# First attention: two groups of heads projected and split, block 1 normalized, before the first scores; the first stack read in halves

## What is computed

```python
def _L0_attn_ref(in_features, Wq, Wk, Wv, Wo):      # 16 heads of 16
    q = split_heads(in_features @ Wq.T)
    k = split_heads(in_features @ Wk.T)
    v = split_heads(in_features @ Wv.T)
    scores = jnp.einsum('bhsd,bhtd->bhst', q, k) * scale
    scores = jnp.where(causal[None, None], scores, -jnp.inf)
    attn = jax.nn.softmax(scores, axis=-1)
    out = jnp.einsum('bhst,bhtd->bhsd', attn, v)
    return out.transpose(0, 2, 1, 3).reshape(B, S, D) @ Wo.T
...
xn = _layernorm(x, axis=-1)
x = x + _L0_attn_ref(xn, ...) + _L0_ffn_ref(xn, ...)     # 8 experts, 2 per token, and a shared one
xn = _layernorm(x, axis=-1)
x = x + _L1_attn_ref(xn, ...) + _L1_ffn_ref(xn, ...)     # a gated linear attention; 8 experts, 2 per token
```

## Time and profile before

| | |
|---|---|
| median of three runs | 1816.02 us (1812.69 to 1818.68) |
| the profiled execution | 1823.78 us, span of its instructions 1821.9 us, mean granted clock 0.942 |
| PE (TensorE, matmuls) busy | 1638.2 us, 90% of the span |
| DVE (VectorE) busy | 869.7 us, 48% |
| ACT (ScalarE) busy | 667.7 us, 37% |
| POOL (GpSimd) busy | 738.1 us, 41% |
| the chain that ended last, by engine | PE 78%, DVE 12%, issue 4% |

### The profile page before, as it was taken

One profiled execution on the slowest core, in us unless ns is written; L12 is line 12 of the kernel. 1 busy time (PEld: TensorE's weight loads), 2 busy tenths in 40 slices (PEclk: granted clock), 3 DMA queues, 4 the chain that ended last, 5 costly groups with the idle time before them and its releaser, 6 DMA issues.

```text
span 1821.9 us, 32039 instructions
## 1 busy us (share of the span) xinstructions
PE 1638.2 (90%) x10912; PEld 1214.3 (67%) x10912; DVE 869.7 (48%) x2492; ACT 667.7 (37%) x1617; POOL 738.1 (41%) x845
## 2 busy tenths in 40 slices
PE   3798988988887999999988578999899999999997
PEld 2344534444443799999755345656899999999997
DVE  3866787667650232322165797988322112222221
ACT  1344444445452122222353334432433333333332
POOL 3122223455551055555542237885233333333332
PEclk8789988989897999999999789999999999999999
DMA  7533433252404122222351255435622222222221
GB/s 203 117 90 95 97 84 76 54 106 64 95 5 163 66 72 72 71 73 70 117 162 58 73 174 117 97 70 123 240 36 36 38 36 39 36 36 35 37 40 22
DMA packets 79739, 149.98 MB, mean 82 GB/s; under 512 B 13125, under 2 KB 61377, under 8 KB 73441
## 3 DMA queue, kind: packets, MB, share of 16 engines
q1 hardware_dynamic: 55040, 110.56, 23.2%
q0 software_dynamic: 24544, 37.38, 9.5%
HBM read 103.05 MB, written 44.45 MB: 81 GB/s over the span
## 4 chain that ended last, share of the span: by engine, by line
PE 78%; DVE 12%; issue 4%; ACT 2%; DMA 2%; POOL 1%; SPq 0%; DVEq 0%; ACTq 0%; POOLq 0%
PE PS L1413 21%; PE PS L1431 20%; PE PS L1299 5%; DVE PS L1717 5%; PE PS L1237 3%; PE PS L1526 3%; PE PS L1378 3%; PE PS L1387 2%; PE PS L1263 2%; PE PS L1617 2%; PE PS L1398 2%; PE PS L1284 2%; PE PS L1325 2%; PE PS L1536 1%; PE PS L1606 1%
## 5 line engine op out<-in xcount | busy, mean ns | idle before, releaser
L1413 PEld LDWEIGHTS PS<-arena 128*128 128x128 f32 x3408 | 400.7, 193 | 15.8 <-DVE arena L1940 4.5
L1413 PE MATMUL PS<-arena 128*128 128x128 f32 x3408 | 407.5, 277 | 3.1 <-DVE arena L1940 3.1
L1431 PE MATMUL PS<-arena 128*128 x1704 | 392.4, 379 | 0.0
L1431 PEld LDWEIGHTS PS<-arena 128*128 128x128 f32 x1704 | 311.6, 190 | 40.2 <-issue 0.2
L1940 DVE COPY arena<-PS 128x256 f32<-128x256 f32 x142 | 60.3, 425 | 413.2 <-PE PS L1398 402.9
L1717 DVE CUSTOM_DVE_ANT_0 PS<-PS,arena 128x512 f32<-128x512 f32 (+3 forms) x512 | 234.2, 524 | 36.2 <-PE PS L1263 36.0
L866 POOL DMA_INDIRECT out<-arena x71 | 111.6, 1572 | 313.6 <-ACT arena L1087 292.5
L1077 ACT ACTIVATE arena<-PS,arena 128x128 f32<-128x128 f32 x568 | 162.4, 368 | 138.2 <-PE PS L1413 138.2
L1016 ACT ACTIVATE arena<-PS 128x512 f32<-128x512 f32 (+1 forms) x256 | 166.9, 704 | 89.0 <-PE PS L1284 87.8
L806 POOL TENSOR_SCALAR_AFFINE_SELECT arena<-arena 128x256 f32<-128x256 f32 x256 | 99.0, 411 | 230.8 <-ACT arena L1016 229.4
L852 POOL DMA_INDIRECT arena<-XN,arena x142 | 142.0, 1000 | 122.8 <-PE PS L1398 81.6
(11 more groups left out here) (237 smaller groups left out, 2058.5 us busy)
## 6 DMA issues: line engine op xcount, KB each, us to landing
arena<-FD SPq DMA_DIRECT2D x32, 512.0 KB
arena<-in_w SPq DMA_DIRECT2D x16, 1024.0 KB
SPL<-arena SPq DMA_DIRECT2D x32, 384.0 KB, 2.6
arena<-SPL SPq DMA_DIRECT2D x32, 384.0 KB, 5.3
XN<-arena SPq DMA_DIRECT2D x16, 512.0 KB, 2.9
arena<-SPL SPq DMA_DIRECT2D x32, 256.0 KB, 6.2
arena<-SUM SPq DMA_DIRECT2D x16, 512.0 KB, 5.1
arena<-in_x SPq DMA_DIRECT2D x8, 512.0 KB, 10.1
```

Of the source, the lines that this page charges most:

```text
L1413: ins = pe.matmul(o, m.now[i % 2][:, c * F + 128 * f:c * F + 128 * f + 128], m.xt[i % 2][:, 128 * c:128 * c + 128], start=(c == 0), stop=( ...
L1431: ins = pe.matmul(to, m.hT[i % len(m.hT)][:, 128 * c:128 * c + 128], m.WD[:, bass.ds(e * (nf * 256) + c * 256, 256)], start=(c == 0), stop ...
```

## The change

Six things change.

1. Before the first `scores` the plan now has the projections and cuts of groups 0 and 1, `stack` 0 and 1, both halves of V of block 0, the logits of block 0, and all layer-norm steps of block 1 up to `logitsT`. Group 2's projections enter the waiting list at once, at idx = -10.
2. What ACT, DVE, POOL and SP do behind a projection (bf16 copy, subtraction and cast, low part, write) is a step of its own, `cut` (n, m). For groups 0 and 1 it stands behind both projections. From group 2 on `with_cuts` places it: behind the next `scores`, or, if earlier, ahead of a second small step after the projection or of a `stack`.
3. All four banks are used by turns until idx = 0 (`two_banks`); from there on 7 and 6. The count that `scoresT` of head 0 waits for follows from it (`exp_first`).
4. `stack` 0 is read in two halves, for heads 0 to 3 and 4 to 7 (twelve DMAs). PE waits for the second half at head 4 (`stk_late`). In every group all six reads now wait for both writes.
5. SP issues the loads of x for blocks 2 to 7 before those of Wo, at the start.
6. Since the layer norm is seven steps ahead, `route` and `scatter` begin seven values of idx earlier.

```diff
--- before.py
+++ after.py
@@ -70,7 +70,6 @@
     ln = ln0_steps()
     for _ in range(2):
         out += next(ln)
-    out.append(("first_banks",))
     waiting = []
 
     def later(rank, parts):
@@ -87,20 +86,26 @@
                     continue
             return
 
-    out.extend([("project", 0, 0), ("project", 0, 1), ("stack", 0), ("clear_meta",)])
-    later(0, [("project", 1, 0), ("project", 1, 1), ("stack", 1)])
-    later(3, [("project_v", 0, 0), ("project_v", 0, 1), ("done",)])
+    for n in range(2):
+        out.extend([("project", n, 0), ("project", n, 1), ("cut", n, 0), ("cut", n, 1), ("stack", n)])
+        out.extend([("project_v", 0, 0), ("project_v", 0, 1)] if n else [("clear_meta",)])
+    while out[-1] != ("logitsT", 1):
+        out += next(ln)
     route = iter([("route", p) for p in range(20)] + [("scatter", i, (k,)) for i in range(NT) for k in range(2)])
     clears = iter([("clear", p) for p in range(4)])
     lnleft = True
     for idx in range(-LEAD, NH + 1):
-        if idx % 8 == 5 and 2 <= (idx + 3) // 8 + 2 < NHB:
+        if idx == 1 - LEAD:
+            later(0, [("project", 2, 0), ("project", 2, 1), ("stack", 2)])
+        if idx % 8 == 5 and 3 <= (idx + 3) // 8 + 2 < NHB:
             later(0, [("project", (idx + 3) // 8 + 2, 0), ("project", (idx + 3) // 8 + 2, 1), ("pause",)])
-        if idx % 8 == 0 and 2 <= idx // 8 + 2 < NHB:
+        if idx % 8 == 0 and 3 <= idx // 8 + 2 < NHB:
             out.append(("stack", idx // 8 + 2))
         if idx == NH - 6:
             out.append(("bias_rows",))
         lead = idx + LEAD
+        if idx == 0:
+            out.append(("two_banks",))
         if 0 <= idx < NH:
             out.append(("scoresT", idx // 8, idx % 8))
             step()
@@ -129,9 +134,34 @@
         step()
     out += list(route)
     out.append(("slots",))
+    return with_cuts(out)
+
+
+def with_cuts(steps):
+
+
+    out, left = [], []
+
+    def flush():
+        out.extend(("cut",) + c for c, _ in left)
+        left.clear()
+
+    for step in steps:
+        small = step[0] in SMALL or step[0] == "values" or step == ("route", 15)
+        if left and (step[0] == "stack" or (small and left[0][1])):
+            flush()
+        out.append(step)
+        if small:
+            left[:] = [(c, True) for c, _ in left]
+        if step[0] == "project" and step[1] >= 2:
+            left.append((step[1:], False))
+        if step[0] == "scores":
+            flush()
+    assert not left
     return out
 
 
+SMALL = ("xt0", "xt1", "logits", "logitsT", "project", "project_v", "maxrow", "scale", "unscaleT", "output")
 CLOSE = ("stack", "maxrow", "unscaleT", "pause", "done")
 
 
@@ -247,11 +277,12 @@
 def attention_banks(order):
 
 
-    uses, ring, first = Uses(), [4, 5, 6, 7], True
+    uses, ring = Uses(), [4, 5, 6, 7]
     for step in order:
-        if step[0] == "first_banks":
-            ring, first = [7, 6], False
-        elif step[0] in ("xt0", "xt1", "logits", "logitsT", "project", "project_v", "maxrow", "scale", "unscaleT", "output"):
+        if step[0] == "two_banks":
+            ring = [7, 6]
+            uses.at[step] = tuple(uses.count[b] for b in (4, 5))
+        elif step[0] in SMALL:
             ring.append(ring.pop(0))
             uses.take(step, ring[-1])
         elif step[0] == "values":
@@ -487,6 +518,7 @@
 
         plan0 = attention_order()
         banks0 = attention_banks(plan0)
+        exp_first = banks0.pop(("two_banks",))
         plan1 = shared_order()
         plan2 = second_order()
         scat_all = 32 * (NT // 4)
@@ -509,6 +541,7 @@
         spl_out = [[sem(f"spl_out{n}{m}") for m in range(2)] for n in range(3)]
         stk_in = [[sem(f"stk_in{n}{m}") for m in range(2)] for n in range(3)]
         max_in = [sem(f"max_in{n}") for n in range(3)]
+        stk_late = [sem(f"stk_late{m}") for m in range(2)]
         v_made, s_made, s_max = sem("v_made"), sem("s_made"), sem("s_max")
         max_cut, max_turned = sem("max_cut"), sem("max_turned")
         const0_set, p_cut = sem("const0_set"), sem("p_cut")
@@ -583,6 +616,8 @@
             x_load(1)
             sp.dma_start(WRV[:, :, :], t["Wg"]).then_inc(wr_in, 16)
             sp.dma_start(WV[:, :, :], t["Wv"]).then_inc(wvo_in, 16)
+            for b in range(2, NB):
+                x_load(b)
             heads = t["Wo"].rearrange("(j r) g n -> j r g n", r=32)
             for g in range(4):
                 lo = 64 * (g % 2)
@@ -596,18 +631,22 @@
                 sp.wait_ge(lo_cut, 2 * n + m + 1)
                 if n >= 3:
                     sp.wait_ge(stk_in[n % 3][m], 48 * (n // 3))
+                if n == 3:
+                    sp.wait_ge(stk_late[m], 48)
                 sp.dma_start(SPL[n % 3, m].rearrange("k p s -> p k s"), PT[m]).then_inc(spl_out[n % 3][m], 16)
 
             def stack(n):
                 for m in range(2):
                     sp.wait_ge(spl_out[n % 3][m], 16 * (n // 3 + 1))
-                    if n >= 3:
-                        sp.wait_ge(st_made, 16 * (n - 2))
-                        sp.wait_ge(s_made, 24 * (n - 2))
-                    parts = SPL[n % 3, m].rearrange("k (d j) s -> k d (j s)", j=8)
-                    for sl, part, many in SLOTS[m]:
-                        dst = STK[n % 3][m][16 * sl:16 * (sl + many), :, :].rearrange("p j s -> p (j s)")
-                        sp.dma_start(dst, parts[part:part + many]).then_inc(stk_in[n % 3][m], 16)
+                if n >= 3:
+                    sp.wait_ge(st_made, 16 * (n - 2))
+                    sp.wait_ge(s_made, 24 * (n - 2))
+                for lo, hi in ((0, 4), (4, 8)) if n == 0 else ((0, 8),):
+                    for m in range(2):
+                        parts = SPL[n % 3, m].rearrange("k (d j) s -> k d (j s)", j=8)
+                        for sl, part, many in SLOTS[m]:
+                            dst = STK[n % 3][m][16 * sl:16 * (sl + many), lo:hi, :].rearrange("p j s -> p (j s)")
+                            sp.dma_start(dst, parts[part:part + many, :, S * lo:S * hi]).then_inc(stk_late[m] if lo else stk_in[n % 3][m], 16)
 
             def maxrow(n):
                 bk, use = banks0["maxrow", n]
@@ -643,13 +682,10 @@
             for kind, *a in plan0:
                 if kind == "norm":
                     norm0(*a)
-                elif kind == "project":
+                elif kind == "cut":
                     split_out(*a)
                 elif kind == "stack":
                     stack(*a)
-                    if a[0] == 0:
-                        for b in range(2, NB):
-                            x_load(b)
                 elif kind == "maxrow":
                     maxrow(*a)
                 elif kind == "bias_rows":
@@ -1256,6 +1292,9 @@
                 h = 8 * n + j
                 pe.wait_ge(stk_in[n % 3][0], 48 * (n // 3 + 1))
                 pe.wait_ge(stk_in[n % 3][1], 48 * (n // 3 + 1))
+                if h == 4:
+                    pe.wait_ge(stk_late[0], 48)
+                    pe.wait_ge(stk_late[1], 48)
                 for i in (3, 2, 0, 1):
                     w, o = 128 * (i + 1), OFF[i]
                     if h and i != 0:
@@ -1280,7 +1319,7 @@
                     if h:
                         pe.wait_ge(p_made, 2 * (h - 1) + (1 if kb == 0 else 2))
                     elif kb:
-                        pe.wait_ge(bank[(4, 5)[kb == 2]], 1)
+                        pe.wait_ge(bank[(4, 5)[kb == 2]], exp_first[kb == 2])
                     ins = pe.matmul(ps(3, o, o + w), k[0:99, j, 128 * kb:128 * kb + 128], q[0:99, j, 128 * kb:512], start=True, stop=True)
                     if kb in (0, 2):
                         ins.then_inc(st_made)
@@ -1697,7 +1736,7 @@
                 dve.tensor_copy(META[:, :, 0, 1], token).then_inc(const0_set)
                 dve.tensor_scalar(META[:, :, 1, 1], token, float(SECOND), None, ALU.add).then_inc(const0_set)
 
-            def project(n, m):
+            def cut(n, m):
                 bk, use = banks0["project", n, m]
                 dve.wait_ge(hi_cut, 2 * n + m + 1)
                 dve.tensor_tensor(R1[m][:, :], ps(bk, 0, 512), PT[m][:, CUTS[m][0], :], ALU.subtract).then_inc(bank[bk])
@@ -1907,8 +1946,8 @@
                     logits_turn(*a)
                 elif kind == "clear_meta":
                     clear_meta()
-                elif kind == "project":
-                    project(*a)
+                elif kind == "cut":
+                    cut(*a)
                 elif kind == "scores":
                     scores(*a)
                 elif kind == "split":
```

## The result

The changed kernel takes 1828.62 us (median of 7 runs, 1823.29 to 1835.74), the kernel before 1814.90 (7 runs, 1811.98 to 1818.68): a ratio of **1.0078**, 95% interval 1.0058 to 1.0099, so 14 us slower. It lies outside the range of 1804 to 1827. The profiled execution took 1835.74 us, span 1833.9.

What follows compares the result with a forecast made beforehand. DVE's small work was taken to set the pace up to 98 us, PE from there to 500. Terms -6 + 3 + 1.5 + 1 + 0 = -0.5 put 1816.0 at 1815.5 us; own range 1811 to 1821, with rivals 1804 to 1827.

Steps and rivals of the forecast that it cites:

- term 5: PE's clock in the groups with projections: some ten falls of six to seven us before, no net change, 0.
- Term 1: The front: first scores 7.8 us later, but head 16 0.9 earlier and 5.0 us of PE work ahead; together -6.
- Term 2: Groups 3 to 5, small step between projections: delayed cuts make PE wait, 1.0 us a group, +3.
- Terms 3 and 4: Other ten groups: stall moves from scores to `scale`, 0.15 each, +1.5; POOL's later low parts and masks delay `values`, +1.
- Rival D: Clock falls in all 13 groups because the longer idle pieces leave none out; +8, 1823.5 us; chance 0.10.
- A: Faster: the front's gain stays and the groups give nothing back; 1810, or 1804 if two groups' clock holds; chance 0.33.
- B: Slower: stall in front of `scale` comes on top, 0.9 us net in each of 13 groups, +12; 1825; chance 0.12.
- C: First scores start at 31.5 us, when the stack's first half is there; some 1805 us; chance 0.00.
- one sign of failure: PE idle from 98 to 500 us off the 51 us before by more than 5 would show the forecast wrong.

Runs made afterwards that it cites:

- e2: Changed kernel with the routing started behind head 43 again instead of head 36; 1819.03 us, ratio 1.0009 to the kernel before.
- e10: Changed kernel with routing behind head 43 and delayed cuts in groups 2 to 5 only; 1820.97 us, ratio 1.0034 to the kernel before.
- e11: The kernel before, unchanged, run again for one more profile; 1811.77 us, ratio 1.0015.
- e6: The kernel before with only the routing started eight heads later, behind head 51 instead of 43; 1818.47 us, ratio 1.0047.
- e1: Changed kernel with each cut from group 2 on right behind its projection again; 1828.86 us, ratio 1.0066 to the kernel before.
- e7: Changed kernel with the first stack read whole and the loads of x behind it, as before; 1832.96 us, ratio 1.0115 to the kernel before.
- e9: Changed kernel with only the large routing steps 14 to 19 put back behind heads 57 to 62; 1828.96 us, ratio 1.0081 to the kernel before.
- e12: The kernel of e9, unchanged, run again for one more profile; 1820.35 us, ratio 1.0051 to the kernel before.
- e3: Changed kernel with cuts right behind their projections and routing behind head 43, leaving the new front and halves; 1822.30 us, ratio 1.0019 to the kernel before.
- e4: The kernel before with only the cuts of groups 2 and later delayed behind the next scores; 1826.79 us, ratio 1.0051.
- e5: The kernel before with delayed cuts in groups 2 to 5 only; 1811.42 us, ratio 1.0011.
- e8: Changed kernel with block 1's steps out of the front, routing behind head 43, delayed cuts in groups 2 to 5 only; 1813.76 us, ratio 1.0019 to the kernel before.

## Why the prediction was wrong

The table takes the intervals between milestones from the 14 profiled executions (mean, with lowest and highest), and sets kernels with and without a feature against each other.

| What differs | Stretch | With it | Without it | Cost |
|---|---|---|---|---|
| new front (delayed cuts, routing behind head 43) | to maxrow 5 | 233.0 (e2, e10: 233.1, 232.8) | 231.2 (before, e11, e6: 228.9 to 233.6) | +1.7 |
| routing steps 0 to 13 from head 36 | maxrow 1 to 5 | 137.2 (after, e1, e7, e9, e12: 136.1 to 139.2) | 132.0 (e2, e3, e10: 131.6 to 132.8) | +5.2 |
| steps 14 to 19 between maxrow 5 and 6 | maxrow 5 to 7 | 71.7 (after, e1, e7: 71.0 to 72.3) | 67.2 (e2, e3, e9, e10, e12: 66.6 to 68.0) | +4.5 |
| delayed cuts from group 6 on | maxrow 7 to 15 | 236.7 (after, e2, e4, e7, e9, e12: 233.6 to 240.4) | 229.8 (before, e1, e3, e5, e8, e10, e11: 226.9 to 233.4) | +6.9 |

The sum is 18.3 us; maxrow 15 comes at 548.5 in the changed kernel and e7, and at 529.3 in the kernel before and e11, which is 19.2. The ratios of the whole time say 14 (after) and 21 (e7).

The table says what happens inside the attention, and for the delayed cuts the whole time does not follow it. On the old front it does: e4's ratio is 0.40% over e5's, 7 us, for the cuts from group 6 on. On the new front e1, without delayed cuts, has maxrow 15 at 538.6, 8 and 12 us ahead of the changed kernel and e7, and is only 2 us faster than the change; e3 and e10 are no faster than e2 by their ratios, though their maxrow 15 comes earlier (533.4 and 528.2 for 534.7). The stretch behind maxrow 15 takes 1277 to 1294 us in the 14 profiles, which is as wide as what is looked for, and 1291.7 and 1294.2 in e1 and e10. Why is open. What both views agree on is the routing: 9.7 us by the table, 7 to 12 by the whole time.

**The step that is missing: the routing, +9.7 us, costed nowhere.** I counted that the plan "is then seven layer-norm steps further on" and took the PE work of these steps as a gain. I did not ask what takes their places in the list. The large steps cost 4.5 us because of where they fall, as e6 shows on the other kernel. The small ones cost in another way. PE's rows from maxrow 1 to 5, of the changed kernel and then of e10:
```profile
99.00:238.20 139.20, 119.14 (x738) 64.11 (x737) 97.28 (x426) 59.40 (x98) 33.55 (x74) 0.90 0.37 88
```
```profile
101.20:232.80 131.60, 113.15 (x737) 61.31 (x737) 93.32 (x371) 59.26 (x97) 33.29 (x73) 0.96 0.39 93
```
DVE has 4 us more to do. PE's matmuls are the same, its idle time grows by only 1.4 us (19.7 for 18.3), and yet it is busy for 6.0 us more, at a clock of 0.90 for 0.96. No other pair is so far apart in clock; on average of the five and the three profiles PE is busy 3.5 us more (117.7 for 114.2) and idle 1.5 more. Over the five profiles with the early steps the clock is 0.90 to 0.93, and 0.95 to 0.96 over the three without. The means are 0.918 and 0.953; that is 0.035 x 137 / 0.5, or some 10 us more at the lower level, one or two falls of the six to seven us that term 5 counted. Why the falls come there is not shown by a run of its own.

**Term 1, -6, measured +1 to +4 by group 5.** The chain was right in its parts (V's copy at 32.01 for 31.7, scores at 43.98 for 42.2; 1.2 of the 1.8 us are the norm, 2.55 us long where the row that I took has 1.38). Two things in its second half failed. The base, head 16's scores at 97.08, was one execution; maxrow 1 came at 99.3 in it, and at 97.7 and 95.6 in the two others with this plan there, so the front was 3.8 us late at maxrow 1 (101.3 in the six profiles with the new front and delayed cuts), not 0.9 early. And of the 5.0 us of work ahead only half came back. From maxrow 1 to 5, with delayed cuts on both sides, the new front takes 132.8 and 131.6 us (e2, e10) and the old one 135.4 and 133.9 (e4, e5); without them 131.6 (e3) against 134.3, 133.5 and 133.3 (before, e11, e6). That is 2.5 and 2.1 us less: PE is busy 2.7 and 3.2 less, and idle 0.1 and 1.2 more. Why its busy time does not fall by the whole 5.0 is not shown. With the late start counted in, maxrow 5 is 1.0 us later on the new front with delayed cuts (233.0 for 232.0) and 4.3 later without (235.5 for 231.2), so the +1.7 of the table holds a gain of the delayed cuts on this front.

**Term 2, +3.** Groups 2 to 5 pay nothing for the delayed cuts: maxrow 5 comes at 233.0 with them and at 235.5 without (e3) on the new front, and at 230.9 and 233.0 (e4, e5) against 231.2 on the old one. Of the waits that I worked out, the one in front of the second projection was too large: 2.3 us each, and measured are 0.9 and 0.5, where the kernel before has three of some 0.5. The second ones, of 2.0 us in front of a transpose and a turn of the logits, came (1.9 expected). That a head that goes first is worth as much where DVE has its layer norms to do is my reading; no run separates it.

**Terms 3 and 4, +2.5 for all groups, measured +6.9 for seven.** The mechanism was right and its size was not. `scale` waits 2.42 (I had 2.5). What is saved is 2.0 a group (20.1 less 5.9, by seven), as worked out; but I also took `maxrow`'s wait as gone and the chain behind as even. The idle time as a whole says otherwise: 31.0 to 35.7 us in the six profiles with delayed cuts, 23.4 to 26.5 in the seven without, on average 8.7 more or 1.2 a group where I had 0.15 and a little for POOL. PE is busy 2.0 us less in return (201.7 for 203.7 us).

**Term 5, the clock, 0.** For the delayed cuts it holds: 0.91 to 0.94 from maxrow 7 to 15 with them, 0.90 to 0.92 without, in spite of pieces of 2.42 us. Rival D, all 13 groups falling, is refuted there. The Trainium skill's page "TensorE: Matmul & The Clock Gate" says in its section "A second HAM failure mode: psum-queue depth-cycling" (the prediction names the section ahead of it) that frequent micro-idles between groups of matmuls that cycle through PSUM banks make the clock swing. By that alone the delayed cuts should have cost clock; no profile here shows it for the pieces in front of `scale`, while the small routing steps, which add 1.4 us of idle time in pieces, do go with a lower one.

**The rivals.** A fell with term 1. B (+12 us for 13 groups) named the right stall, and its 0.9 us a group is close to the 1.0 measured; but the wait that it left in place went, the clock did not fall, and without the routing it gives no 14 us. C is refuted by order in the changed kernel, and e8 shows that its 31.5 (32.02 measured) would have been worth nothing. I had taken one sign of failure as a test: idle time from 98 to 500 us off by more than 5. It is off by 14, and it pointed at the right place.

None of the three versions made from this (e5, e8, e10) beats the kernel before.
